# Exchanging the sides of two narrow weight products, with three rearrangements, in a four-layer attention and adapter kernel

## The reference

```
x = x + L0(x)     # q, k, v; RMS norm and rotation of q and k; k, v written into a paged cache of
                  # blocks of 16; attention over a window of 256 keys behind each token; times Wo
x = x + L1(x)     # for each sequence one of 8 matrices 64x64, which mixes the tokens
x = x + L2(x)     # base weight and adapter, one of 4 of rank 16 for each sequence, with the
                  # weights Wt ahead of the adapter's A and Wp behind its B
x = x + L3(x)     # base weight W and adapter, one of 8 of rank 16 for each sequence
```

## Time and profile before

| what | us |
|---|---|
| median of 3 runs | 427.21 |
| the runs | 427.21, 427.32, 425.41 |
| the profiled execution | 422.87 |
| its span, from the first to the last instruction | 421.1 |
| TensorE busy (share of the span) | 409.3 (97%) |
| VectorE | 308.1 (73%) |
| GpSimd | 258.2 (61%) |
| ScalarE | 240.8 (57%) |
| the projections end at | 103.43 |
| window 4's key transposes start at | 159.94 |

### The profile page before, as it was taken

The page is one execution under the profiler, slowest core; times in us unless marked ns, Lnnn a source line. Parts: engine busy times, 40 slices in busy tenths (PEclk is TensorE's granted clock), DMA queues, the critical chain, the costliest instruction groups (busy, mean ns, idle before and its releaser), DMA issues.

```text
span 421.1 us, 9975 instructions
## 1 busy us (share of the span) xinstructions
PE 409.3 (97%) x2942; PEld 315.8 (75%) x2942; DVE 308.1 (73%) x901; ACT 240.8 (57%) x611; POOL 258.2 (61%) x230
## 2 busy tenths in 40 slices
PE   5999999999999988999999999999999999999997
PEld 1586877888945566888787878878778778888776
DVE  3798768769478586967978779687786787967742
ACT  4383433433267465756767567666676666765741
POOL 3206775275579877777777777777767777662000
PEclk9999999999999999999999999999999999999999
DMA  6616565157584455656555656565565655653321
GB/s 177 218 51 195 170 179 182 53 168 260 157 267 119 149 148 149 180 154 175 163 138 166 169 161 165 140 180 156 147 177 141 171 160 137 186 144 99 109 69 61
DMA packets 74107, 65.15 MB, mean 155 GB/s; under 512 B 50277, under 2 KB 52453, under 8 KB 74055
## 3 DMA queue, kind: packets, MB, share of 16 engines
q1 hardware_dynamic: 55088, 38.09, 31.3%
q0 software_dynamic: 15456, 22.08, 19.7%
q10 hardware_dynamic: 3510, 4.35, 2.9%
HBM read 74.46 MB, written 11.93 MB: 205 GB/s over the span
## 4 chain that ended last, share of the span: by engine, by line
PE 82%; DMA 5%; DVE 4%; POOL 4%; issue 4%; ACT 1%; SPq 0%; POOLq 0%; DVEq 0%; ACTq 0%
PE banks L1151 37%; PE banks L1141 11%; PE banks L1315 11%; PE banks L1294 9%; PE banks L1331 4%; PE banks L1167 3%; PE banks L1354 3%; PE banks L1344 2%; DMA wpt_late<-newkv,idx_all 1%; DMA newkv<-kvo 1%; POOL q_roots L497 1%; POOL wpt_late L524 1%; POOL windows L524 1%; DMA windows<-newkv,idx_all 1%; DMA xt_s<-xt_dram 1%
## 5 line engine op out<-in xcount | busy, mean ns | idle before, releaser
L524 POOL DMA_INDIRECT windows<-kvrows_dram,idx_all x78 | 83.0, 1064 | 31.1 <-issue 24.0
L524 POOL DMA_INDIRECT windows<-newkv,idx_all x78 | 81.8, 1049 | 29.0 <-issue 22.6
L655 ACT ACTIVATE pt_s<-banks 112x384 f32<-112x384 f32 x128 | 56.0, 496 | 61.9 <-PE banks L1141 56.9
L649 ACT ACTIVATE prob<-prob,negmax 128x336 f32<-128x336 f32 x128 | 72.4, 566 | 24.4 <-DVE negmax L1011 24.4
L1011 DVE CUSTOM_DVE_ANT_0 prob<-banks,mask 128x336 f32<-128x336 f32 x128 | 57.4, 503 | 2.7 <-PE banks L1294 1.2
L1021 DVE TENSOR_SCALAR prob<-prob,rinv 128x336 f32<-128x336 f32 x128 | 47.1, 410 | 2.3
L1294 PE MATMUL banks<-kt_s,qt_s 64*128 64x336 f32 x256 | 44.8, 468 | 0.0
L1315 PEld LDWEIGHTS banks<-pt_s,windows 112*64 112x64 f32 x624 | 33.3, 136 | 13.4 <-issue 10.9
L1315 PE MATMUL banks<-pt_s,windows 112*64 112x128 f32 x624 | 42.7, 279 | 0.0
L1151 PE MATMUL banks<-wf_hi,x 128*128 128x512 f32 x120 | 41.1, 403 | 0.0
L1141 PE MATMUL banks<-ident_r,prob_w 128*112 128x128 f32 x384 | 40.4, 242 | 0.0
(11 more groups left out here) (222 smaller groups left out, 918.2 us busy)
## 6 DMA issues: line engine op xcount, KB each, us to landing
usel<-utab SPq DMA_DIRECT2D x64, 128.0 KB
xt_s<-xt_dram SPq DMA_DIRECT2D x16, 256.0 KB, 3.7
newkv<-kvo SPq DMA_DIRECT2D x16, 256.0 KB, 2.6
stage<-xtok_dram SPq DMA_DIRECT2D x16, 256.0 KB, 11.3
tsel<-ttab SPq DMA_DIRECT2D x64, 64.0 KB
out_dram<-xo ACTq DMA_DIRECT2D x15, 256.0 KB
windows<-kvrows_dram,idx_all POOLq DMA_INDIRECT x78
windows<-newkv,idx_all POOLq DMA_INDIRECT x78
```

The source lines that it names most:

```text
L524: P.indirect_dma_start(kv_s[i][:, c, :], None, newkv if new else kvrows, bass.IndirectOffsetOnAxis(ap=idx_all[:, new * CH + c, b:b + 1], a ...
L649: A.activation(pr, pr, ACT.Exp, bias=negmax[:, g:g + 1], scale=-1.0, accum_out=psum_p[b % 2][:, g:g + 1]).then_inc(S["exp_done"], 1)
L655: A.activation(pt_s[g][:], tb[g % 2][0:KP, 0:CH * 128].rearrange("p (c q) -> p c q", c=CH), ACT.Copy).then_inc(S["pt_ev"], 1)
```

## The change

Four edits. The two narrow products exchange sides: the 64 narrow columns are now the weights and the 512 wide ones stream, so that each product makes 64 rows by 512 columns; the one with Wp goes to partitions 0 to 63 of a bank and the one with Wt to 64 to 127, by turns. ScalarE takes the 128 x 512 result out (`thin`, which shares its place with the work tile `t2`), four transposes bring it back to the layout that is used further on, and what read the two old results reads the transposed ones. The transposes stand between two halves of the adapter product, and `ct` moves behind it. VectorE's `combined_of` (which waits for `ct`) moves behind the low part of the adapter table. In GpSimd's list the new rows of window 3 go ahead of the old rows of window 4, and the new rows of window 4 stand behind the old rows of window 5. The sync queue reads one number for each tile, in which VectorE has packed the indices of both sequences, and takes it apart with register arithmetic. The values of a window are one block of 24 instructions, behind `mix`.

```
-            turned(bank[4], wpt_s, b2_s, 64).then_inc(S["up_mm"], 1)
             pe.wait_ge(S["l_wt"], 16 * C)
-            pe.wait_ge(S["q_raw"], TILES)
-            pe.wait_ge(S["q_sq"], TILES)
-            turned(bank[5], wt_s, a2_s, 64).then_inc(S["t2_mm"], 1)
+            for c in range(C):
+                for h, narrow, wide in ((0, b2_s, wpt_s), (1, a2_s, wt_s)):
+                    last = mm(bank[4][64 * h:64 * h + 64], narrow[:, c, :], wide[:, c, :], start=(c == 0), stop=(c == C - 1))
+            last.then_inc(S["thin_mm"], 1)
...
             queries_t(0)
-            pe.wait_ge(S["up_ev"], 1)
             pe.wait_ge(S["l_low3"], 32)
-            dense(bank[4][:, 0:64], lambda c: a3_s[:, c, :], lambda c: upt[:, c, 0, :]).then_inc(S["ct_mm"], 1)
             pe.wait_ge(S["rows_ready"], 1)
             pe.wait_ge(S["wb_ident"], 1)
-            turned(ob, wbn_s, a3_s, 128).then_inc(S["t3_mm"], 1)
+            turned(ob, wbn_s, a3_s, 128, (0, 1))
+            pe.wait_ge(S["thin_ev"], 1)
+            pe.wait_ge(S["q_raw"], TILES)
+            pe.wait_ge(S["q_sq"], TILES)
+            for k in range(C):
+                last = turn(bank[5][:, 128 * k:128 * k + 128], thin_w[:, 128 * k:128 * k + 128])
+            last.then_inc(S["thin_t"], 1)
+            turned(ob, wbn_s, a3_s, 128, (2, 3)).then_inc(S["t3_mm"], 1)
+            pe.wait_ge(S["up_ev"], 1)
+            dense(bank[4][:, 0:64], lambda c: a3_s[:, c, :], lambda c: upt[:, c, 0, :]).then_inc(S["ct_mm"], 1)
```

ScalarE, VectorE (its new wait in `query_first`, and the packing), GpSimd, the sync queue, and TensorE's values:

```
             query_ev(end)
-            evac(upt[:], bank[4][:, 0:256]..., "up_mm", "up_ev")
+            act.wait_ge(S["q_n"], 1)
+            act.wait_ge(S["k_n"], PAIRS)
+            evac(thin, bank[4][:], "thin_mm", "thin_ev")
             split_high(0)
-            evac(t2tab[:, :, :, 0]..., bank[5][:, 0:256]..., "t2_mm", "t2_hi")
-            evac(ct[:], tb[0][:, 0:64], "ct_mm", "ct_ev")
-            split_high(1)
...
             queries_ev(0)
+            evac(upt[:], thin_turned(0)..., "thin_t", "up_ev")
+            evac(t2tab[:, :, :, 0]..., thin_turned(1)..., "thin_t", "t2_hi")
+            split_high(1)
             evac(t3tab[:, :, :, 0]..., "t3_mm", "t3_hi")
+            evac(ct[:], tb[0][:, 0:64], "ct_mm", "ct_ev")
...
+                if t == 1:
+                    dve.wait_ge(S["thin_t"], 1)
...
+                link(V.tensor_copy(adf[:, 2, :], subj_s[:]))
+                link(V.scalar_tensor_tensor(adf[:, 0, :], adf[:, 1, :], float(NE2), adf[:, 0, :], ALU.mult, ALU.add))
+                link(V.scalar_tensor_tensor(adf[:, 2, :], adf[:, 0, :], 8.0, adf[:, 2, :], ALU.mult, ALU.add))
+                two = adf[:, 2, :].rearrange("a (t u) -> a t u", u=2)
+                V.scalar_tensor_tensor(picks[:], two[:, :, 1], float(PICKS), two[:, :, 0], ALU.mult, ALU.add).then_inc(S["meta_ready"], 1)
...
-            for k in range(NB):
-                if k == 0:
-                    pool.wait_ge(S["comb_ev"], NE3 // 2)
-                    gather(4, 0)
-                    continue
-                if k + 2 < NB:
+            gather(3, 1)
+            pool.wait_ge(S["comb_ev"], NE3 // 2)
+            gather(4, 0)
+            pool.wait_ge(S["pv_mm"], 1)
+            gather(5, 0)
+            gather(4, 1)
+            for k in range(2, NB - 2):
+                if k > 2:
                     gather(k + 2, 1)
...
+                both = sp.value_load(picks[0:1, t:t + 1], min_val=0, max_val=PICKS * PICKS - 1)
+                pick = [both % PICKS, both // PICKS]
                 for u in range(2):
-                    s = sp.value_load(subj_s[0:1, 2 * t + u:2 * t + u + 1], min_val=0, max_val=7)
+                    s = pick[u] % 8
...
-                    a2 = sp.value_load(ad2_s...)
-                    a3 = sp.value_load(ad3_s...)
-                    a23 = sp.value_load(pair_s...)
+                    a23 = pick[u] // 8
+                    a2, a3 = a23 % NE2, a23 // NE2
...
-                    values(k, 0)
                     if t >= 1:
                         mix(t - 1)
-                    values(k, 1)
+                    values(k)
```

More of the change, by code:

```diff
@@ L149, in build @@
         adf = sb("adf", [1, 3, NB])
-        pair_s = sb("pair_s", [1, NB], i32)
+        picks = sb("picks", [1, TILES], i32)
+        PICKS = 8 * NE2 * NE3
         pos = sb("pos", [128, TILES])
@@ L165, in build @@
         half = sb("half", [128, 16])
-        t1, t2 = sb("t1", [128, 8, 64]), sb("t2", [128, 8, 64])
+        t1 = sb("t1", [128, 8, 64])
+        [thin_w] = words([("thin_w", [128, 512])])
+        t2 = sb("t2", [128, 8, 64])
+        thin = t2[:].rearrange("p h d -> p (h d)")
         wt_tok, wt_ge = (t[0:NB].rearrange("p h d -> p (h d)")[:, 0:NW * BLOCK] for t in (t1, t2))
@@ L307, in kpair, with thin_turned @@
             return banks[:, 2 * (i % 2):2 * (i % 2) + 2]
+        def thin_turned(h):
+            return bank[5].rearrange("p (c h r) -> p c h r", c=C, h=2)[:, :, h]
         def qbank(t):
@@ L981, in _, with combined_of @@
             split_low(1)
-            dve.wait_ge(S["ct_ev"], 1)
-            V.tensor_tensor(ctm, ct[:].unsqueeze(1).to_broadcast([128, NE3, 64]),
-                            con("of3").unsqueeze(2).to_broadcast([128, NE3, 64]), ALU.mult).then_inc(S["ct_ev"], 1)
+            def combined_of():
+                dve.wait_ge(S["ct_ev"], 1)
+                V.tensor_tensor(ctm, ct[:].unsqueeze(1).to_broadcast([128, NE3, 64]),
+                                con("of3").unsqueeze(2).to_broadcast([128, NE3, 64]), ALU.mult).then_inc(S["ct_ev"], 1)
             def b3_split():
@@ L998, in _ @@
                 ob[:].rearrange("p (c e r) -> p c e r", c=C, e=NE3), "t3_hi", 1, "t3_ev")
+            combined_of()
             def mask_at(b):
@@ L1230, in _, with turned @@
                     index_win()
-            def turned(to, w, r, n):
-                for k in range(C):
+            def turned(to, w, r, n, chunks):
+                for k in chunks:
                     last = dense(to[:, n * k:n * k + n], lambda c: w[:, c, 128 * k:128 * k + 128], lambda c: r[:, c, :])
@@ L1303, in probs_t, with values @@
                 last.then_inc(S["pt_mm"], 1)
-            def values(b, p):
+            def values(b):
                 t, u = b // 2, b % 2
@@ L1309, in values @@
                     pe.wait_ge(S["wf_ev"], 1)
-                pe.wait_ge(S["pt_ev"], 4 * b + 2 * p + 2)
-                for c in range(CH):
-                    for h in range(2):
-                        g = 2 * p + h
-                        col = 256 * u + 128 * p
-                        last = mm(ob[64 * h:64 * h + 64, col:col + 128], kv_s[b % WINDOWS][:, c, 256 + 64 * g:320 + 64 * g],
-                                  pt_s[g][:, c, :], start=(c == 0), stop=(c == CH - 1))
-                if p == 1:
-                    last.then_inc(S["pv_mm"], 1)
+                for p in range(2):
+                    pe.wait_ge(S["pt_ev"], 4 * b + 2 * p + 2)
+                    for c in range(CH):
+                        for h in range(2):
+                            g = 2 * p + h
+                            col = 256 * u + 128 * p
+                            last = mm(ob[64 * h:64 * h + 64, col:col + 128], kv_s[b % WINDOWS][:, c, 256 + 64 * g:320 + 64 * g],
+                                      pt_s[g][:, c, :], start=(c == 0), stop=(c == CH - 1))
+                last.then_inc(S["pv_mm"], 1)
             def project(t):
```

15 lines of the change are left out of this document (5 added, 10 removed).

## The result

The changed kernel takes 434.73 us (median of 4 runs, 432.53 to 437.35) beside 426.41 for the kernel before (425.41 to 427.32): a ratio of 1.0198, interval 1.013 to 1.0266. A median here holds every run, a ratio leaves out the runs more than 1.5% above the fastest of the same kernel, so the two need not divide out. It is slower by 8.3 us, and the forecast was 2.3 us faster. The profiled execution took 433.80 us, of which 431.9 is the span: 10.8 us more than the 421.1 of before.

What follows compares the result with a forecast made beforehand. Front until 159.94 us bound by GpSimd's gather list, tiles after it by TensorE. Values -1.9 and gathers -0.4 sum to -2.3 us: 424.9 us from a median of 427.21, likely 423.9 to 425.5, range 422.6 to 427.3.

Steps and rivals of the forecast that it cites:

- the picks: Sync queue: seven of eight register loads per tile give way to register arithmetic; nobody waits for the loads behind, value 0.
- the rivals: Five alternatives: gathers landing mildly late 0.25, early 0.15, residual late 0.08, gathers much later 0.06, clock falling 0.03.
- The values: Tiles after 159.94: one block of 24 instructions saves 0.14 us a tile, 1.9 us in all; bounds 0 and 2.2.
- The narrow products: Front: products fall from 7.07 to 3.7 us, transposes 0.4, but waiting near 121 takes the gain: 0, bounds -0.3, +0.5.
- The gathers: Front, windows 3 and 4: the wait at 149.49 goes, window 4 takes it back; -0.4 us, from -2.9 to +3.4.
- The clock rival: Front: TensorE's longer waits before 121 and 160 drop its clock to 1.2 GHz; +0.6 us, 427.8; chance 0.03.

Runs made afterwards that it cites:

- tsel_off: Kernel before with an unused tile of 16 words right ahead of `tsel`, which alone moves 64 bytes: 432.53 us, ratio 1.0168.
- aligned: Changed kernel with the tile `picks` 32 words long instead of 16, so all tiles behind it stand where they were: 423.90 us, ratio 0.9961.
- nopicks: Changed kernel with the eight register loads for each tile as before, without the packed index: 425.86 us, ratio 0.9979.
- narrow: Kernel before with the narrow products exchanged and nothing else: 427.69 us, ratio 1.0022.
- spread_al_three: Changed kernel with `picks` at 32 words, each `usel` load issued as two of 16 partitions, and narrow products as before: 421.79 us, ratio 0.9902.
- spread_aligned: Changed kernel with `picks` at 32 words and each `usel` load issued as two of 16 partitions: 419.42 us, ratio 0.9882.
- spread_al_fill: As `spread_aligned`, with two products of 512 columns whose result nobody reads ahead of the key transposes near 121: 419.68 us, ratio 0.9863.
- usel_back: Changed kernel with an unused tile of 16 words right ahead of `usel`, putting everything from `usel` on back in place: 425.16 us, ratio 0.9972.
- rest_back: Changed kernel with an unused tile of 16 words right behind `usel`, putting only what lies behind it back in place: 424.89 us, ratio 0.9938.
- tsel_back: Changed kernel with an unused tile of 16 words right ahead of `tsel`, putting `tsel` alone back in place: 427.13 us, ratio 1.0022.
- before_spread: Kernel before with each `usel` load issued as two loads of 16 partitions and nothing else: 423.21 us, ratio 0.9935.

## Why the prediction was wrong

**The step that failed** is the one on the picks: "Nobody waits for the loads behind them: after 159.94 TensorE waits for no table. Value: 0 in itself". It failed twice over.

It counted the edit's instructions and not its tile. The tile of half the length is part of the change, and none of the rivals was about a place in memory. `tsel_off` puts its price at 1.68% (1.13 to 2.23), some 7 us of 426; that is most of the 8.3 us, and with the forecast's own gain counted in, of some 10.

And it read "no wait" as "not near". In the kernel before the last `usel` of the first tile had been issued by 155.51 (153.98 + 1.53, the next row of the sync queue's timeline behind the earlier trace rows), and `up` starts at 167.63: 12.1 us. In the changed kernel the same interval, from 159.65 (154.86 + 4.79) to the landing at 171.58, is 11.9 us. With `tsel` at its place it is 10.9 us in `aligned` (157.28 to 168.13) and 11.4 in `nopicks` (160.46 to 171.86). So the margin was 0.2 to 1.3 us at these rates, an estimate from these rows, and loads that start 3.8 to 4.5 us later can use it up: `nopicks` has the first wait without the packed index. A landing of over 10 us was reason enough to work the margin out.

**The sum.** Of the 10.8 us of span, 9.3 are the waits for `usel`. The values give about 1.9 back, so some 3.4 are left, a remainder. The clock's falls behind two of the six waits account for nearly all of it: beyond the wait and the 17.17 us of a tile without one, the tile with the wait of 3.83 us is 1.93 us longer (166.21 to 189.14), and that with the wait of 2.02 us is 1.33 longer (329.81 to 350.33). Behind the wait of 2.67 us the clock stayed at 1.00; two instructions of `up` tell the two cases apart, 0.70 us and 1.19:

```profile
296.92 0.70 PE L1384 MATMUL banks<-usel,zh 128*128 128x512 f32 x2 [2.67 <-DMA usel<-utab]
...
333.36 1.19 PE L1384 MATMUL banks<-usel,zh 128*128 128x512 f32 x2 [2.02 <-DMA usel<-utab]
```

**The narrow products**: right in their own time, 3.58 us forecast as 3.7, transposes 0.38 as 0.4. That the gain is worth nothing was argued from a gather that lands when it did, and this landing moved. With the exchange the store of the last keys, from which the gathers start, lands in 3.82 us where it took 5.61:

```profile
108.30 3.82 DMA newkv<-kvo
```

So the key transposes start 16.39 us behind the start of the narrow products (104.86 to 121.25) and not 17.61 (103.43 to 121.04): 1.2 us are gained there, and the projections, which ended 1.4 us later in this execution, hide it. It is 16.0 to 16.6 us in all 13 profiled kernels with the exchange, and 17.5 or more wherever TensorE waits there without it; why the store gets shorter isn't shown. The shorter list and the sooner landing leave a wait of 2.22 us and not 3.4, and behind it the clock's fall takes about 1.6 us, more than was gained. In the end no gain can be told (`narrow` 1.0022; `spread_al_three` against `spread_aligned`); against `spread_al_fill` of the same session, where the clock stayed up, `spread_al_three` is 2.1 us slower, with intervals that just overlap. A value of zero is not refuted, but the reason given for it is.

**The gathers**: right in the number, by luck. The wait at window 3 is gone (0.16 us at 150.12, put down to nothing that the profile shows), and window 4 takes it back, at 159.97 for a forecast of 159.5. But the forecast kept GpSimd's slots and took 5.0 us from the last issue to the landing. With the store landed sooner the last issue came at 152.05, 2.2 us ahead of 154.28, and the landing took 7.9 us, more than the bound of 7.1; the two errors cancel. The wait there is 0.36 us and not 2 to 3, since TensorE came later: the clock's fall near 121 had cost it about 1.6 us (`fold(0)` starts at 126.73, before at 124.90; 0.2 of the difference is the landing at 121.25). In the profiled execution of `aligned` window 4 is transposed at 158.76 and not waited for.

**The values**: right. 24 instructions in 1.46 us behind the mixing product, and 17.17 us for a tile without waits (189.14 to 206.31, from one block of values to the next but one) where it was 17.30 (191.47 to 208.77): 0.13 us a tile for a forecast of 0.14. The list of waits holds none of a mixing product.

**The clock rival**: a small chance, and it did occur, at the other of the two waits it named and behind two of the six waits for `usel`. In the front its price was taken up at window 4, as the forecast's own logic has it; in the tiles it added to a cost that had another cause.

With `tsel` at its place the whole change lies at 0.9961 (`aligned`), 0.9972 (`usel_back`), 0.9938 (`rest_back`) and 1.0022 (`tsel_back`); the forecast, 424.9 for 427.21, is 0.9946. Three of the four intervals hold it and that of `tsel_back` (0.9981 to 1.0062) doesn't, and TensorE still waits 0.9 to 6.2 us for `usel` in these four. So the place alone doesn't bring the forecast back for certain. With the loads out of the way on both sides the four edits are worth 0.9935 less 0.9882, 0.53% or 2.3 us, for a forecast of 2.3; the intervals are 0.3 and 0.7% each way, so this is agreement and no proof, and agreement of the total, not of its steps.

## What to carry to other kernels

An edit includes its allocations: when a tile changes its size, ask what lies behind it and who writes there, and keep the destination of small pieces where it was with a tile of the old length. A load that nobody waits for still needs its margin worked out, from its issue to its use, and the number of DMA engines that carry it. And to tell a program's effect from its place, add an unused tile to the kernel before: it costs one run.

## What the runs showed of the hardware

- Moving the destination of 128-byte pieces by 64 bytes, from a multiple of 128 to an odd multiple of 64, cost 1.68% of a whole kernel (1.13 to 2.23), seen not in the recorded time of packets but as waits of 7.0 us rather than 0.9 for the loads behind them on the same queue. The same move of `usel` and the tiles ahead of it left the time at 0.9938 (0.9898 to 0.9978), though its profiled execution waits 6.2 us; a move of the window buffers from an odd multiple of 32 to a multiple of 512 made no difference that could be told.
- A load with a repeated dimension of 2 as its slowest kept as many engines busy as two (13.1% of 16) and took up to 12.91 us to land; issued as loads of 16 rows it was never waited for, and the kernel before was 0.65% faster (0.37 to 0.93). Gathers of new keys beside such loads landed 5.6 to 7.9 us behind their last issue, and within 3.3 us in `spread_al_three`, beside spread ones.
- Behind a wait of 2.22 us for a gather TensorE ran at 0.50 for some 3 us. The length of the wait doesn't decide it: behind the one of 1.45 us in `before_spread` the clock fell, behind the 2.35 of `tsel_back` and the 2.67 at 296.92 it stayed at 1.00.
